# Output stage of a two-layer model tower: gate rounds moved behind other work, channel sums as trees of adds

## What is computed

```python
out = q + ln_fwd(Z1_bar, ttt_norm_scale, ttt_norm_bias)   # per head
...
mu = Z.mean(-1, keepdims=True)
var = Z.var(-1, keepdims=True)                            # over all 768 channels
Zn = (Z - mu) * jax.lax.rsqrt(var + LN_EPS) * post_norm_scale + post_norm_bias
gate = jax.nn.gelu(x @ wg)
return Zn * gate @ wo
```

## Time and profile before

| | us |
|---|---|
| median of three executions | 1385.31 |
| lowest, highest | 1383.65, 1391.73 |
| the profiled execution, its time | 1388.91 |
| its span, first to last instruction | 1387.1 |
| output stage in it, first product to last `res` | 825.7 to 1067.2 |
| of that, up to the last tile's masked products | 825.7 to 1027 |

### The profile page before, as it was taken

The page is one execution under the profiler, slowest core; times in us unless marked ns, Lnnn a source line. Parts: engine busy times, 40 slices in busy tenths (PEclk is TensorE's granted clock), DMA queues, the critical chain, the costliest instruction groups (busy, mean ns, idle before and its releaser), DMA issues. The chain is left out here.

```text
span 1387.1 us, 29176 instructions
## 1 busy us (share of the span) xinstructions
PE 1260.8 (91%) x11347; PEld 864.8 (62%) x11347; DVE 922.0 (66%) x2230; ACT 709.6 (51%) x1513; POOL 380.4 (27%) x445
## 2 busy tenths in 40 slices
PE   4889999799789999899999989889976899899999
PEld 3433333355557777677777767777764445588888
DVE  6588888423587778798888878887884899400001
ACT  1446555432224443688888864767664334343310
POOL 6500000100057776556666640000000234300000
PEclk9989999969989999999999999999997999999999
DMA  3342121200113324634343542212101300077721
GB/s 97 102 126 69 47 63 31 74 13 1 39 54 123 117 83 138 208 102 131 95 138 100 150 115 58 58 41 63 41 0 64 156 1 1 35 257 283 284 70 46
DMA packets 99285, 127.41 MB, mean 92 GB/s; under 512 B 24589, under 2 KB 87804, under 8 KB 94956
## 3 DMA queue, kind: packets, MB, share of 16 engines
q1 hardware_dynamic: 96556, 123.44, 29.0%
q0 software_dynamic: 1536, 1.59, 0.5%
q10 hardware_dynamic: 1056, 0.52, 0.1%
HBM read 89.06 MB, written 37.88 MB: 92 GB/s over the span
## 5 line engine op out<-in xcount | busy, mean ns | idle before, releaser
L1792 POOL TENSOR_SCALAR r_grD<-gr 32x192 f32<-32x192 f32 x192 | 101.8, 530 | 93.5 <-PE bank L1523 44.8
L700 ACT ACTIVATE PT<-bank 128x1024 f32<-128x1024 f32 x96 | 94.3, 1022 | 59.5 <-PE bank L580 58.7
L641 DVE TENSOR_REDUCE mx<-bank 128x1 f32<-128x512 f32 x176 | 110.0, 681 | 12.2 <-PE bank L563 11.9
L1523 PE MATMUL bank<-r_grD,ek 128*128 128x256 f32 x384 | 100.0, 396 | 0.0
L2538 DVE TENSOR_TENSOR eo_all<-bank,m_b2s 128x768 f32<-128x768 f32 x8 | 7.7, 958 | 138.5 <-PE bank L2499 138.5
L2530 ACT ACTIVATE x_g<-bank,m_b1s 128x128 f32<-128x128 f32 x192 | 51.4, 399 | 75.7 <-PE bank L2481 75.7
L2412 POOL TENSOR_SCALAR m_xs<-m_xs 128x256 f32<-128x256 f32 x4 | 2.5, 631 | 263.4 <-DVE m_xs L2303 263.4
L1523 PEld LDWEIGHTS bank<-r_grD,ek 128*128 128x128 f32 x384 | 67.7, 189 | 9.3
L1736 ACT ACTIVATE r_t<-r_xh,r_cd 128x64 f32<-128x64 f32 x192 | 70.0, 427 | 0.7
L1514 PEld LDWEIGHTS bank<-gr,r_A 128*128 128x128 f32 x384 | 47.6, 190 | 33.4 <-DVE gr L1686 31.6
L1352 POOL TENSOR_TENSOR rope_c<-cy,p_rope 128x512 f32<-128x512 f32 x48 | 60.0, 1272 | 20.0 <-DVE cy L1205 20.0
(11 more groups left out here) (375 smaller groups left out, 3230.4 us busy)
## 6 DMA issues: line engine op xcount, KB each, us to landing
wb<-in_m_w SPq DMA_DIRECT2D x32, 1152.0 KB, 5.3
ek<-k_d SPq DMA_DIRECT2D x32, 384.0 KB
k_d<-t_late SPq DMA_DIRECT2D x46, 256.0 KB, 2.8
tgt<-c_d SPq DMA_DIRECT2D x33, 196.0 KB
c_d<-t_late SPq DMA_DIRECT2D x32, 196.0 KB, 2.9
g_d<-gr SPq DMA_DIRECT2D x32, 192.0 KB
o_G<-g_d SPq DMA_DIRECT2D x32, 192.0 KB, 3.0
qk_d<-a_parts SPq DMA_DIRECT2D x24, 192.0 KB, 3.0
```

The costliest lines, as they stand in the source:

```text
L641: v.tensor_reduce(mx[u % 2][:, j // 4, j % 4:j % 4 + 1], slot(f"A{u}.{j}"), AX.X, ALU.max).then_inc(*dve.did(f"max{u}.{j}"))
L700: a.activation(PT[kt % 2][:, 2 * hp:2 * hp + 2, :], STB[s % 2][:, :, :], ACT.Exp, scale=DH ** -0.5)\
L1523: last = t_.matmul(SP_[g][:, i * B * E1:(i + 1) * B * E1], ek[r][:, p, :], grD[g][:, i, :, :].rearrange("p b e -> p (b e)"), start=False, ...
L1792: last = g_.tensor_scalar(grD[g][rr, :, b, :], b3(gr[j % RING][rr, cols(g)]), 0.0, None, ALU.bypass)
```

## The change

Three edits in `ttt_output`. Gate round 1 moves behind the masked products on TensorE, and its gelu behind `sq` and `zc` on ScalarE. Round 2 moves from the even iteration to the odd one that follows (`late_pair`), behind the output product on TensorE and behind `zc` on ScalarE; SP's token loads wait there too. Since rounds of one pair now lie in two iterations, the table is changed twice as often. The two sums over channel blocks become three adds each, of three blocks to three, then two, then one, through a free tile of the recurrence (`r_g2`). GpSimd stays without work.

```diff
+        late_pair = lambda i: (i - 3) // 2 if i % 2 and 0 <= i - 3 < TILES else None
...
+        part3 = M["r_g2"][:, :].rearrange("p (c n) -> p c n", c=PH)
...
             @block.sync
...
-                    k = pair_of(i)
+                    k = late_pair(i)
                     if k is not None and k + 2 < TILES // 2:
                         sp.wait_ge(*pe.at(f"g2.{k}"))
...
             @block.tensor
...
-                    if k is not None:
-                        gates(k, 1)
                     if (n := at(i, 0)) is not None:
                         t_.wait_ge(*dve.at(f"Sm1_{n}"))
...
                         last.then_inc(*pe.did(f"Z{n}"))
+                    if k is not None:
+                        gates(k, 1)
...
-                    if k is not None:
+                    if (k := late_pair(i)) is not None:
                         gates(k, 2)
...
             @block.vector
...
-                        v.tensor_reduce(s1[:, :], x[n % 4][:, :, :].rearrange("p c n -> p n c"), AX.X, ALU.add).then_inc(*dve.did(f"s1_{n}"))
+                        v.tensor_tensor(part3, xx[:, 0:PH, :], xx[:, PH:HP, :], ALU.add).then_inc(*dve.did(f"s1a{n}"))
+                        v.wait_ge(*dve.at(f"s1a{n}"))
+                        v.tensor_tensor(s1[:, :], part3[:, 0, :], part3[:, 1, :], ALU.add).then_inc(*dve.did(f"s1b{n}"))
+                        v.wait_ge(*dve.at(f"s1b{n}"))
+                        v.tensor_tensor(s1[:, :], s1[:, :], part3[:, 2, :], ALU.add).then_inc(*dve.did(f"s1_{n}"))
                     if (n := at(i, 2)) is not None:
                         v.wait_ge(*act.at(f"sq2_{n}"))
+                        v.wait_ge(*dve.at(f"s1_{n + 1}" if n + 1 < TILES else f"s2_{n - 1}"))
+                        v.tensor_tensor(part3, sq2[:, 0:PH, :], sq2[:, PH:HP, :], ALU.add).then_inc(*dve.did(f"s2a{n}"))
...
             @block.scalar
...
-                    if k is not None:
-                        gelu(k, 1)
                     if (n := at(i, 0)) is not None:
                         a.wait_ge(*pe.at(f"Z{n}"))
...
                     if k is not None:
+                        gelu(k, 1)
+                        a.preload_act_table_set("natural_log_exp_and_others")
+                    if (k := late_pair(i)) is not None:
                         gelu(k, 2)
                         a.preload_act_table_set("natural_log_exp_and_others")
```

More of the change, by code:

```diff
@@ L1851, in steps @@
                 for n, lag in parts:
-                    if n[0] == "g":
+                    if n == "g2":
+                        names += [f"{n}.{late_pair(i)}"] if late_pair(i) is not None else []
+                    elif n[0] == "g":
                         names += [f"{n}.{pair_of(i)}"] if pair_of(i) is not None else []
@@ L1856, in steps @@
             return names
-        pe = Steps(sem("o_pe"), steps(("S0_", 0), ("V", 1), ("m", 2), ("g0", 0), ("S1_", 0), ("vp", 3), ("W", 0), ("g1", 0), ("Z", 0),
+        pe = Steps(sem("o_pe"), steps(("S0_", 0), ("V", 1), ("m", 2), ("g0", 0), ("S1_", 0), ("vp", 3), ("W", 0), ("Z", 0), ("g1", 0),
                                       ("y", 4), ("g2", 0)))
         dve = Steps(sem("o_dve"), steps(("res", 5), ("Sm0_", 0), ("xc", 2), ("Sm1_", 0), ("yg", 4), ("x1_", 1), ("xr", 3), ("x2_", 1),
-                                        ("s1_", 1), ("s2_", 2)))
-        act = Steps(sem("o_act"), steps(("sc", 4), ("ln", 1), ("rs", 1), ("sq2_", 2), ("lp", 3), ("rp", 3), ("g0", 0), ("g1", 0),
-                                        ("sq", 0), ("zc", 0), ("g2", 0)))
+                                        ("s1a", 1), ("s1b", 1), ("s1_", 1), ("s2a", 2), ("s2b", 2), ("s2_", 2)))
+        act = Steps(sem("o_act"), steps(("sc", 4), ("ln", 1), ("rs", 1), ("sq2_", 2), ("lp", 3), ("rp", 3), ("g0", 0),
+                                        ("sq", 0), ("zc", 0), ("g1", 0), ("g2", 0)))
+        part3 = M["r_g2"][:, :].rearrange("p (c n) -> p c n", c=PH)
         with nc.Block() as block:
@@ L2037, in _ @@
                     if (n := at(i, 1)) is not None:
+                        xx = x[n % 4][:, :, :]
                         v.wait_ge(*dve.at(f"x1_{n}"))
                         for p in range(HP):
-                            last = v.scalar_tensor_tensor(x[n % 4][:, p, :], x[n % 4][:, p, :], bC[:, p:p + 1], q_of(n)[:, p, :],
-                                                          ALU.add, ALU.add)
+                            last = v.scalar_tensor_tensor(xx[:, p, :], xx[:, p, :], bC[:, p:p + 1], q_of(n)[:, p, :], ALU.add, ALU.add)
                         last.then_inc(*dve.did(f"x2_{n}"))
                         v.wait_ge(*dve.at(f"x2_{n}"))
-                        v.tensor_reduce(s1[:, :], x[n % 4][:, :, :].rearrange("p c n -> p n c"), AX.X, ALU.add).then_inc(*dve.did(f"s1_{n}"))
+                        v.tensor_tensor(part3, xx[:, 0:PH, :], xx[:, PH:HP, :], ALU.add).then_inc(*dve.did(f"s1a{n}"))
[3 more added lines that the diff above has]
+                        v.tensor_tensor(s1[:, :], s1[:, :], part3[:, 2, :], ALU.add).then_inc(*dve.did(f"s1_{n}"))
                     if (n := at(i, 2)) is not None:
                         v.wait_ge(*act.at(f"sq2_{n}"))
+                        v.wait_ge(*dve.at(f"s1_{n + 1}" if n + 1 < TILES else f"s2_{n - 1}"))
+                        v.tensor_tensor(part3, sq2[:, 0:PH, :], sq2[:, PH:HP, :], ALU.add).then_inc(*dve.did(f"s2a{n}"))
                         if n:
                             v.wait_ge(*pe.at(f"vp{n - 1}"))
-                        v.tensor_reduce(s2[:, :], sq2[:, :, :].rearrange("p c n -> p n c"), AX.X, ALU.add).then_inc(*dve.did(f"s2_{n}"))
+                        v.wait_ge(*dve.at(f"s2a{n}"))
+                        v.tensor_tensor(s2[:, :], part3[:, 0, :], part3[:, 1, :], ALU.add).then_inc(*dve.did(f"s2b{n}"))
+                        v.wait_ge(*dve.at(f"s2b{n}"))
+                        v.tensor_tensor(s2[:, :], s2[:, :], part3[:, 2, :], ALU.add).then_inc(*dve.did(f"s2_{n}"))
             @block.scalar
```

## The result

The changed kernel takes 1375.74 us in the median of 4 runs (1372.88 to 1379.08) against 1388.52 (1383.65 to 1396.3): ratio 0.9892, 95% interval 0.9857 to 0.9927. Twelve more executions, compared with 17 of the kernel before, gave 0.9935 (0.9906 to 0.9964). Forecast were 11.5 us less, 0.9917. The profiled span fell from 1387.1 to 1371.1 us, 16.0, of which the output stage explains 12.9: from its first score product to the next stage's first product it took 241.9 us (825.74 to 1067.65) and takes 229.0 (823.79 to 1052.83). It began 1.95 us earlier and what follows it was 1.2 shorter, and nothing was changed in either; in the twelve profiles of this study, all of kernels equal up to there, the stage began between 823.8 and 832.1.

A forecast was written before the change was run, and what follows sets the result against it. TensorE's waits for `h` and gelu 0 were taken to bound the body, a chain the tail. Body 11.4 us less tail 0.8 gave 10.6, plus 0.9 of clock: 11.5 less, 1373.8 us from median 1385.3; range 1368 to 1380.

The forecast's parts named there:

- Pair 24.6: Output stage body: one pair of tiles falls from 26.98 us to 24.6, by 0.54 + 1.83 = 2.37 us.
- no order goes below: TensorE, body: without its two losses a pair takes 24.11 us, which TensorE itself needs whatever the order.
- -1.1: First pair's gate round 2, now in tile 3, delays tile 4 by 1.1 us.
- The tail: Tail chain from last round 1 through ScalarE's loads: 13.6 us in place of 12.8, a loss of 0.8.
- the sum of 0.9 for the clock: Output stage: of 3.4 us lost at half clock in body and tail, 0.9 counted as regained.
- Gain 0.54 us per pair: Even tile: round 1 behind the masked products waits 0.50 us for gelu 0 in place of 1.04.
- gain 1.83 us: Round 2 in the odd tile: the even tile's mean product no longer waits for `h`, 1.83 us per pair.
- Rival D: Mean product held by something other than `h`; only round 1's term and the tail count: about 3 us, 1382; chance 0.03.
- Gain in the body 0: Sums as trees on VectorE: about 0.55 us saved per tile, but no gain in the body once round 2 moved.
- A: Clock gives back more: both half-clock stretches go, none comes, all 3.4 us count; 1371 or less; chance 0.18.
- B: ScalarE replaces VectorE as holdup: chain 1 us longer than forecast, pair 25.6 us, time 1380; chance 0.12.
- C: Table loads hold ScalarE's work behind gelu 2: 17 us per microsecond per load; with 1.38 more each, 1398; chance 0.03.

The follow-up runs named there:

- the run with the chain cut: Changed kernel with gate rounds re-placed so none waits for the gelu before it, first pair's round 2 in its even tile: 1367.31 us, ratio 0.985 to the kernel before.

## Why the prediction held, and where its steps didn't

*The time.* 1373.8 was forecast, 1375.7 measured, 12.9 us less in the stage for 10.6 plus 0.9 of clock. The likeliest case was the one that came. That the whole times lie only 2 us apart owes something to chance: the kernel before had 1385.3 when the forecast was made and 1388.5 beside the changed one, and the second comparison gives 0.9935 where 0.9917 was forecast.

*The sum, term by term.* Up to the last variance product 11.4 us were forecast, and 12.8 came: the start cost 2.8 in place of 1.1, the pair of tiles 4 and 5 gave 1.0 in place of 0.7, the five pairs behind it 2.53 each in place of 2.37, and the half-clock stretch of the kernel before, which is gone, gave 1.9. The tail changed by 0.1 in place of 0.8.

*Pair 24.6.* Measured 24.45. Both waits were read rightly: 1.83 went, and round 1 waits 0.61 for the 0.50 of the walk, since its chain was 9.29 us and TensorE reached it 8.79 into the tile. But "no order goes below" 24.11 was wrong. Without its waits TensorE needs some 23.8 us for a pair: 24.45 less the 0.68 between masked products and round 1, 25.67 less 1.83 in the run with round 1 alone, 24.26 less 0.44 ahead of the second score product in the run with the chain cut. What a product costs from start to start depends on what stands around it (round 1 takes 1.93 us ahead of the masked products, 929.62 to 931.55 in the kernel before, and 1.83 ahead of the output products, 926.01 to 927.84 in the changed one), which a walk over one order doesn't show. The floor too high by 0.3 and the wait too low by 0.1 nearly cancel.

*The start.* "-1.1" for the first pair's round 2 was too small: tile 4 came 1.4 us later in the profile without half clock there, and 2.8 in the other, of which the clock made 1.4.

*The tail.* Forecast 0.8 longer; from the last variance product to the next stage it was 38.6 before, and 38.5 and 40.4 in the two profiles of the changed kernel, so the runs don't decide this term. The last round 0 is back at full clock, as I expected, and new half clock stands elsewhere (round 1 at 1023.81 takes 3.78 us), which the sum of 0.9 for the clock allowed for. The new waits of 5 us (5.65 and 5.19) are not "as long as old ones there", as the prediction has it: the longest old one is 3.67.

*The terms of the edits.* Here the working fails though its sum holds. "Gain 0.54 us per pair" for round 1 and "gain 1.83 us" for round 2 are what stalls were worth in the new order, not what the edits do. Alone round 1 gives 1.31 and round 2 costs 0.7; their stage effects, -6.7 and +8.6, add to +1.9, and together they give -11.9. The reason stands in the prediction's own rows. As long as the mean product waits 1.83 us for `h`, TensorE reaches round 1 after gelu 0's chain, and moving round 1 removes its whole wait; once that wait is gone, the chain is late, and moving round 2 gives 1.23 (25.67 to 24.44). Rival D, which had only round 1's term, was priced wrongly for the same reason.

*The trees.* "Gain in the body 0": shown, 24.44 against 24.45, and the 0.7 us to spare with the old sums was there (0.66 in the run without trees, 13.44 less 12.28 and the 0.50 of `h`). The saving was put too high: two trees in a tile save 0.31 us, not 0.55. The prediction's own terms give 0.42 (2.82 less twice 1.20). By its upper bound of 1.74 a sum, with the hand-overs, a tile would have lost 0.8, which the 0.7 wouldn't have covered; the adds measured stayed well below it.

*Rivals.* A asked for both half-clock stretches to go and none to come. Both went (980.19 in the body, round 0 in the tail), but others came in tile 3 and in the tail, so it did not come about. B and C are out: ScalarE's chain was measured where forecast, and three loads in a row show no drain. D is out, since no row names `h` any more. The drain of 1.38 us per switch that the Trainium skill gives ("ScalarE: Activation LUTs", What ACT_TABLE_LOAD costs) is in no run here; its 1283 ns for the load is what every row shows, the 32 of the changed stage among them. C's slope can't be read off cleanly: 34 us for 16 loads contain the clock.

What stays open is why the same wait costs the clock in one execution and not in another.

## What to carry to other kernels

In a loop where three engines hand work around, price the new order as a whole, by carrying starts from row to row: a move that pays 1.2 us beside another costs 0.7 us alone. A wait on TensorE is dearer than its length when the clock falls behind it, so look at the durations after a wait before you price an edit that makes one longer. When a stage starts at times that wander by more than the effect, compare stages between two fixed instructions, and compare their parts too, since two deviations can cancel in the whole.

## What the runs showed that I had not expected

A wait of 2.06 us repeated in every pair took the granted clock of the products behind it towards its lower level, 1.2 GHz (2.77 in place of 1.99 us, mean clock 0.70), five times in five, where one of 1.66 did so once in five, in the kernel before and in the run with round 1 alone; filling it with useless products gave 10.5 us back. Loads of the activation tables in a row follow each other at 1.29 us.
